# A fused two-layer attention kernel on one core: five seams reordered, the first context half put ahead of a batch's first scores in cross-attention, and a third fold of self-attention's sums on GpSimd

## The reference

```python
# layer 0: cross-attention to a projected memory, gated, then a norm
mem = einsum('bme,de->bmd', memory, W_mem)
ctx = softmax(x @ mem.T / sqrt(512)) @ mem
gate = sigmoid(concat([x, ctx]) @ W_gate + b_gate)
x = rmsnorm(x + gate * ctx)
# layer 1: each token takes one of two expert weights, chosen by a mask (vm)
q, k, v = split(where(vm, n(x) @ v_qkv, n(x) @ l_qkv)); q, k = rotary(q, k)
x = x + where(vm, c @ v_dense, c @ l_dense)        # c: causal self-attention, 16 heads of 32
x = x + cross(n(x) @ cq_w, context @ ckv_w) @ cdense_w     # 16 heads of 16, 375 keys
x = x + where(vm, mlp_v(n(x)), mlp_l(n(x)))        # silu(gate) * up @ down, 1376 wide
```

## Time and profile before

| | |
|---|---|
| median of 3 runs | 2148.39 us (2144.62 to 2150.19) |
| the profiled execution's own time | 2143.99 us |
| its span, first to last instruction | 2142.2 us |
| TensorE busy | 2093.4 us, 98% of the span |
| VectorE, ScalarE, GpSimd busy | 58%, 49%, 44% |
| mean granted TensorE clock | 0.993 of full speed |

### The profile page before, as it was taken

One profiled execution on the slowest core, in us unless ns is written; L12 is line 12 of the kernel. 1 busy time (PEld: TensorE's weight loads), 2 busy tenths in 40 slices (PEclk: granted clock), 3 DMA queues, 4 the chain that ended last, 5 costly groups with the idle time before them and its releaser, 6 DMA issues.

```text
span 2142.2 us, 40674 instructions
## 1 busy us (share of the span) xinstructions
PE 2093.4 (98%) x16042; PEld 1805.2 (84%) x16042; DVE 1237.3 (58%) x1908; ACT 1050.2 (49%) x1877; POOL 943.5 (44%) x773
## 2 busy tenths in 40 slices
PE   8999999999999999999999999989999999999998
PEld 7899998888777778887888888878888888888888
DVE  6665547657589975456666666663434435344343
ACT  5444435343378865534666565553443434433334
POOL 2211127776668854551111211115455554555447
PEclk9999999999999999998999999999999999999999
DMA  6443435655666655567877777745335343443334
GB/s 248 140 158 115 144 134 177 228 204 212 212 202 181 186 189 216 227 201 212 238 235 210 226 217 222 207 132 188 116 122 174 112 140 111 131 142 118 115 89 134
DMA packets 155742, 373.00 MB, mean 174 GB/s; under 512 B 40384, under 2 KB 61216, under 8 KB 145824
## 3 DMA queue, kind: packets, MB, share of 16 engines
q1 hardware_dynamic: 136400, 310.18, 45.8%
q0 software_dynamic: 18720, 60.04, 7.6%
q10 hardware_dynamic: 432, 0.17, 0.0%
HBM read 268.70 MB, written 100.46 MB: 172 GB/s over the span
## 4 chain that ended last, share of the span: by engine, by line
PE 83%; DMA 5%; DVE 3%; POOL 3%; SPq 2%; ACT 2%; issue 1%; POOLq 0%; DVEq 0%; ACTq 0%
PE ps L111 20%; PE ps L113 20%; PE ps L112 20%; PE ps L2017 4%; PE ps L2038 4%; PE ps L2051 3%; PE ps L1332 2%; PE ps L689 2%; PE ps L1321 1%; PE ps L1343 1%; DMA f_arena<-weights 1%; POOL cq_rows L1569 1%; PE ps L1311 1%; DMA cq_rows<-f_arena 1%; ACT f_arena L1595 1%
## 5 line engine op out<-in xcount | busy, mean ns | idle before, releaser
L111 PE MATMUL ps<-r_arena 128*128 128x512 f32 (+6 forms) x2410 | 890.9, 370 | 14.0 <-DVE r_arena L179 8.9
L113 PE MATMUL ps<-r_arena 128*128 128x512 f32 (+6 forms) x2410 | 880.0, 365 | 0.0
L112 PE MATMUL ps<-r_arena 128*128 128x512 f32 (+6 forms) x2410 | 879.6, 365 | 0.0
L179 POOL TENSOR_TENSOR r_arena<-f_arena,r_arena 128x512 fp32r<-128x512 f32 (+1 forms) x434 | 576.7, 1353 | 542.1 <-ACT r_arena L201 397.3
L111 PEld LDWEIGHTS ps<-r_arena 128*128 128x128 f32 (+2 forms) x2410 | 453.1, 188 | 79.0 <-POOL r_arena L179 6.7
L113 PEld LDWEIGHTS ps<-r_arena 128*128 128x128 f32 (+2 forms) x2410 | 452.7, 188 | 64.9
L112 PEld LDWEIGHTS ps<-r_arena 128*128 128x128 f32 (+2 forms) x2410 | 453.7, 188 | 59.3
L201 ACT CAST r_arena<-f_arena 128x512 fp32r<-128x512 f32 x400 | 236.4, 624 | 172.5 <-PE ps L113 127.3
L2159 DVE TENSOR_REDUCE e_negmax<-ps 112x3 f32<-112x1125 f32 (+1 forms) x192 | 229.9, 1198 | 113.1 <-PE ps L2017 113.0
L2476 DVE SCALAR_TENSOR_TENSOR f_arena<-f_arena,ps 128x512 f32<-128x512 f32 (+1 forms) x88 | 57.5, 653 | 233.8 <-ACT f_arena L2363 233.8
L1906 ACT ACTIVATE f_arena<-ps 125x896 f32<-125x896 f32 x192 | 165.4, 915 | 35.6 <-PE ps L2038 33.0
(11 more groups left out here) (215 smaller groups left out, 2575.4 us busy)
## 6 DMA issues: line engine op xcount, KB each, us to landing
f_arena<-weights SPq DMA_DIRECT2D x400, 256.0 KB, 3.0
r_arena<-k_rows SPq DMA_DIRECT2D x192, 188.0 KB, 3.6
k_rows<-r_arena SPq DMA_DIRECT2D x64, 376.0 KB
f_arena<-rows SPq DMA_DIRECT2D x14, 1160.0 KB, 5.2
f_arena<-qk_rows SPq DMA_DIRECT2D x32, 448.0 KB, 4.1
f_arena<-mem_n SPq DMA_DIRECT2D x8, 1536.0 KB, 6.8
f_arena<-mem_e SPq DMA_DIRECT2D x32, 376.0 KB, 4.9
f_arena<-mem_t SPq DMA_DIRECT2D x16, 750.0 KB, 5.5
```

Source lines behind the costliest of these rows:

```text
L111: first = pe.matmul(out, w_hi, x_hi, start=start, stop=False)
L112: pe.matmul(out, w_hi, x_lo, start=False, stop=False)
L113: return first, pe.matmul(out, w_lo, x_hi, start=False, stop=stop)
L179: return engine.tensor_tensor(out, source, high.bitcast(F32), ALU.subtract)
```

## The change

**Setup and phase A.** GpSimd clears the pad block before it turns to work that waits for group 0. VectorE works out the pads' slots in `setup_dve_places`, ahead of the softmax of group 1, and leaves the tiles' jumps (`setup_dve_jumps`) until after it. In group 0 the gate's four steps are interleaved with the four `attended` copies of group 1, which came after the third and fourth step before. For group 1, one half of the normed tokens comes earlier and one piece of splitting later.

**B to C.** The value rows of the last tile count on a semaphore of their own, so GpSimd issues them without waiting for the tile before. The two probability buffers swap places, and the wait for the older scatters passes from batch 0 to batch 1.

**Phase C, every step.** `turn_queries(s + 2)` moves ahead of the transposes on TensorE, and the copy of those queries ahead of the four copies on ScalarE. Block j=1 of the transposes now waits for the copy of these same queries. In 18 of 32 batches GpSimd adds a third fold (112 x 224), and VectorE's sum reads half as much.

**Phase E.** At its head 17 small matmuls that nobody reads (`keep_busy`) are put into three steps, the products for batch 3 are split around the second batch's first scores, and one unit of batch 0 gets another bank. In every step the first context half goes ahead of u=0. At the end the places of the last batch are issued by SyncE and ScalarE, three each, and the transposed maxima of batch 29 come before a context half.

```diff
@@ setup_pool, setup_dve_places @@
                 if m == C_GATE:
+                    pool.memset(tok[:, 0:PADS, :], 0.0).then_inc(pads_zeroed, 1)
...
                     pool.wait_ge(a_m_lo, 2 * CT)
                 ring_low(pool, m)
-            pool.memset(tok[:, 0:PADS, :], 0.0).then_inc(pads_zeroed, 1)
...
+            one_by_one(dve, dve.tensor_tensor(pad_slot[:], pad_m, grid, ALU.add))
+            dve.wait_ge(pads_zeroed, 2)
+            dve.tensor_scalar(tok[:, 0:PADS, ID].bitcast(I32), grid, float(TOKENS), None, ALU.add).then_inc(slots_made, 1)
             dve.wait_ge(s_rank, 2)
             dve.tensor_copy(place, ps[:, 5, 352:366]).then_inc(ranks_made, 1)
+
+        def setup_dve_jumps(dve):
@@ gated @@
+                copies = KT - 1 if g else 0
                 for t in range(KT):
-                    if t == KT - 1 and g + 1 < GROUPS:
+                    if t == copies and g + 1 < GROUPS:
                         for b in range(2):
                             attended(g + 1, b)
...
+                    if g == 0 and t in (1, 2):
+                        attended(1, t + 1)
@@ b_pool @@
+                    done = b_v_scattered if n + 1 < TILES else b_last_scattered.sem
+                    pool.indirect_dma_start(v_rows, ids, b_values(n, j), None).then_inc(done, 16)
...
-            pool.wait_ge(b_v_scattered, 16 * blocks(TILES - 1))
             store_v(TILES - 1)
@@ c_pool, fold @@
+                if b in c_thrice:
+                    pool.tensor_tensor(c_fold, c_half[:, :, 0:quarter], c_half[:, :, quarter:half], ALU.add).then_inc(c_halved.sem, 1)
+                    pool.wait_ge(*c_halved.at(c_halves(b) + 1))
+                    pool.tensor_tensor(c_eighth, c_fold[:, :, 0:quarter // 2], c_fold[:, :, quarter // 2:quarter], ALU.add).then_inc(
+                        c_folded.sem, 1)
@@ c_act @@
+                if s + 2 < BATCHES:
+                    queries(s + 2)
                 if s:
                     for j in range(QUADS):
                         act.wait_ge(c_pt, QUADS * (s - 1) + j + 1)
...
-                if s + 2 < BATCHES:
-                    queries(s + 2)
@@ c_pe @@
-                if j in (1, 2):
-                    pe.wait_ge((c_q, c_k)[j - 1], min(b + 3, BATCHES))
+                if j == 1:
+                    pe.wait_ge(c_q, min(b + 4, BATCHES))
+                if j == 2:
+                    pe.wait_ge(c_k, min(b + 3, BATCHES))
...
+                if s + 2 < BATCHES:
+                    turn_queries(s + 2)
                 if s >= 1:
                     for j in range(QUADS):
                         transposes(s - 1, j)
-                if s + 2 < BATCHES:
-                    turn_queries(s + 2)
@@ c_dve @@
-                dve.tensor_reduce(c_sum[:], c_fold, AX_X, ALU.add).then_inc(c_summed, 1)
+                dve.tensor_reduce(c_sum[:], c_eighth if b in c_thrice else c_fold, AX_X, ALU.add).then_inc(c_summed, 1)
@@ e_sp, e_act @@
+                if b == BATCHES - 1:
+                    place_last(sp, last_places[:3])
+                    return
...
+                if s == BATCHES - 2:
+                    act.wait_ge(e_st, KEY_UNITS * (BATCHES - 3))
+                    place_last(act, last_places[3:])
@@ e_pe @@
+            def keep_busy(bank, count):
+                for _ in range(count):
+                    pe.matmul(ps[0:SEQ, bank, 0:NT], ident_b[0:SEQ, 0:SEQ], causal[:].rearrange("p m s -> p (m s)"),
+                              start=True, stop=True)
...
+                if old:
+                    context(s - 2, 0)
                 if now:
                     scores(s, 0)
...
                 if old:
-                    context(s - 2, 0)
```

More of the change, by code:

```diff
@@ L858, in a_dve @@
                         x_low(g + 1)
-                    means(g - 1, 1)
-                    tokens(g - 1, 0)
+                    if g == 1:
+                        tokens(g - 1, 0)
+                        means(g - 1, 1)
+                        memory_low(g + 1, 1)
+                    else:
+                        means(g - 1, 1)
+                        tokens(g - 1, 0)
                     tokens(g - 1, 1)
@@ L877, in a_dve @@
                     if g == 0:
+                        setup_dve_jumps(dve)
                         setup_dve_slots(dve)
@@ L1166, in c_sp @@
                 load_qk(b)
-            sp.wait_ge(b_v_scattered, 16 * BLOCKS)
+            sp.wait_ge(b_v_scattered, 16 * blocks(TILES - 1))
+            sp.wait_ge(*b_last_scattered.at(16 * tb(TILES - 1)))
             for b in range(3):
@@ L1197, in fold @@
                 if b == 0:
-                    pool.wait_ge(b_v_scattered, 16 * BLOCKS)
+                    pool.wait_ge(b_v_scattered, 16 * blocks(TILES - 1))
+                    pool.wait_ge(*b_last_scattered.at(16 * tb(TILES - 1)))
                 if b:
@@ L1772, in place_queries, with place_last @@
                     e_placed[b].sem, 16)
+        def place_last(engine, parts):
+            b = BATCHES - 1
+            engine.wait_ge(*stored(b))
+            into, done = e_queries[b % 3].rearrange("p t g s -> p t (g s)").bitcast(F32), e_placed[b % 2].sem
+            for t, part in parts:
+                engine.dma_start(rows_of(into, t, part)[:, t], q_rows[b, t, (0, 0, 1)[part]]).then_inc(done, 16)
+        last_places = [(t, part) for t in range(CT) for part in range(3)]
         def e_sp(sp):
@@ L2105, in e_pe @@
                     f_gate_up(pe, 0, 0, 0, (0, 1, 2))
-                if by_key:
+                if by_key and s != BATCHES - 2:
                     maximum_turn(s - 1)
@@ L2116, in e_pe @@
                     scores(s, 2)
-                if new and s:
+                if s == 1:
+                    keep_busy(6, 2)
+                    queries_turn(3)
+                    keep_busy(6, 2)
+                if new and s >= 2:
                     e_key_products(pe, s + 2)
```

78 lines of the change are left out of this document (49 added, 29 removed).

## The result

The changed kernel takes 2153.16 us in the median of 7 runs (2152.68 to 2155.55), the kernel before 2147.28 (2144.62 to 2150.19, 7 runs). The ratio is 1.003, with a 95% interval of 1.0021 to 1.0039: slower by 5.9 us, where the forecast was 2152 with a sum of +3.5. The profiled execution of the changed kernel took 2152.73 us, 8.74 more than the profiled one of before; the medians stand closer because the profiled execution of before lies 3.29 under its kernel's median, and no other execution of it has a trace.

What follows compares the result with a forecast made beforehand. TensorE's program was taken to set the time in phase C. Terms 10.2 - 4.5 - 1.3 - 2.9 + 3.6 - 1.6 = +3.5 us on the median 2148.39 gave 2152 us; 8 in 10 from 2139 to 2163.

Steps and rivals of the forecast that it cites:

- Phase C: Self-attention steps: block j=1 waits for the queries' copy, starting 1.22 us after X, the queries' start; +0.35 a step, +10.2 us.
- The first rival: Phase C: the copy of the queries is hidden after all, gaining 2.9 us; 2139 us, chance 0.20.
- The third: Rival in phase C: TensorE drops to the lower clock, +80 us, to 2230; chance 0.02.
- Phase A: Interleaved copies remove TensorE's stop at 66 us and the load issued at 71.55 quickens without pad scatters beside it; -4.5 us.
- the second rival: Phase A: the load issued at 71.55 stays slow, so the 4.5 us is lost; 2156, up to 2163; chance 0.28.
- B to C: Seam before phase C's first context: value rows scattered earlier, first subtraction moves up too; -1.3 us.
- the 0.84 goes: At the first context of phase C: the 0.84 us wait for value rows disappears because they are scattered earlier.
- Head of E: Start of phase E: added matmuls keep the clock up and places are issued earlier; -2.9 us.
- if the 17 added matmuls keep the clock up: Head of phase E: 1.2 us won in the context and about as much in the products before.
- E's steps: Every step of phase E: hidden wait -0.16, shape changes +0.18, new wait for the maximum +0.13; +3.6 us in all.
- two changes of tile shape: Each step of phase E: the new order adds two shape changes at 0.09 us each, 0.18.
- Tail of E: End of phase E: a context half fills batch 31's 1.37 us wait for places and two engines issue; -1.6 us.

Runs made afterwards that it cites:

- x4: The kernel before with only the new order of queries and transposes in phase C, on TensorE and ScalarE; 2156.28 us, ratio 1.0054.
- x2: The changed kernel with banks 5 and 7 swapped for the second and third block of transposes in phase C; 2144.19 us, ratio 0.999.
- x3: The changed kernel without GpSimd's third fold, VectorE's sum reading what two folds leave; 2153.02 us, ratio 1.0026.
- a2: The kernel before with only phase A's interleaved copies, the pads scattered as late as before; 2149.54 us, ratio 1.0015.
- x6: The changed kernel with all six places of the last batch's queries issued by SyncE again; 2152.99 us, ratio 1.0026.
- x7: The changed kernel without the 17 added matmuls at the head of phase E; 2153.3 us, ratio 1.0034.
- a1: The kernel before with only the setup part, pads cleared, placed and scattered earlier, gate and copies in the old order; 2145.76 us, ratio 0.9998.

## Why the prediction was right

The time, 2153.16, lies 1 us from the forecast, and the sign was right. That it lies so near is in part luck: the forecast started from a median of three runs, 2148.39, 1.1 above the 2147.28 of seven, and its sum of +3.5 was 2.4 under the 5.9 measured; and inside the sum one term missed by 3.5 us and one by 2.2. What carried the sign, the loss in every step of C, was right. By its steps:

- **Phase C: right in place, mechanism and size.** Forecast +0.35 a step and +10.2; measured 0.38 a step and +10.7 (10.6 in x4). The chain of rows gave the start of the second block within 0.01 us (X + 1.22 against 1.23). What it put a little too low was the end: the last block's copy ended at 687.32 + 1.40 = 688.72, X + 3.26 (forecast 3.24), but the context took another 0.38 us behind it, where one quarter of it and the handover had been put at 0.28. In all the context ended 0.12 later than forecast; the rest of the step made good most of it, 0.10 shorter where 0.02 had been taken, so the step's 0.38 beside 0.35 owes something to two errors that cancel. x2 shows that the bank decides, x3 that GpSimd and VectorE don't. The first rival, a hidden copy, is refuted by the bracket itself. The third, a lower clock through the phase, is refuted by the clock of 1.00 in that stretch. The Trainium skill, page "TensorE: Matmul & The Clock Gate", Part 4 on PE-mode transpose, says that transposes don't count as busy in the same way, and this phase with 28 transposes a step and a stall in each doesn't show it.
- **Phase A: right in size, half right in its reason.** Forecast -4.5, measured -4.8 at 90 us. The slow load was there (4.71 from issue at 71.53 to first use in the changed kernel, against 8.97), so the second rival, a load that stays slow, falls. But a2 shows the step that failed: it named the load as the only thing behind TensorE's stop, and the wait for the pad scatters' own landing is another.
- **B to C: right in size, wrong in mechanism.** Forecast -1.3, measured -1.2, and -1.2 to -2.1 in the other eight executions with the new seam. The step that failed is "the 0.84 goes": the first context waits for value rows as before, now for 1.72 us (1.1 to 1.8 in the others). Counted from 575 us, the first of these rows landed 1.2 us sooner, and TensorE was through with its own work 2.1 sooner. The longer stop has a price that the forecast didn't see: behind it the clock fell in x3, x6 and x7 (mean 0.54, 0.77 and 0.77 from 591.5 to 599 us, against 1.00 in the changed kernel's trace), and from the first context to 790 us those three lost 12.3 to 13.7 us in place of 10.7. x4, with the old seam, has such a fall ahead of its first context (0.86 from 590 to 602 us), so it isn't the new seam's alone.
- **Head of E: the term was too large.** Forecast -2.9, measured -0.7, and between executions the head varies by more than that. The step that failed is the price set on "if the 17 added matmuls keep the clock up". They kept it up for a part only: it was 0.50 to 0.53 from 965 to 975 us, 1.00 to 985, and 0.66 from 985 to 990, where the context stands from which the 1.2 was read. Its two halves took 2.04 and 1.29 us there, 0.42 less than the 3.75 from 983.52 to 987.27 in the kernel before (the 3.72 of the earlier trace rows is a row of 92 of the 96 products). And where the clock was up, TensorE waited for other engines.
- **E's steps: right in place and mechanism, near in size.** Forecast +3.6, measured +3.0. Of the parts, the hidden wait was 0.15 (forecast 0.16) and the new wait 0.11 (0.13, in which the handover of 0.05 was taken off where it has to be added). What the forecast called two changes of tile shape, 0.18, shows as 0.09 on the scores by key (0.96 against 0.87) and 0.15 on the parted context halves; that the change of shape is the reason is argued, and no run tests it. The parts come to +0.20, and the step grew by 0.12: what gives 0.08 back in the rest of the step is open.
- **Tail of E: wrong.** Forecast -1.6, measured +1.9. The step that failed is that it looked at the wait for batch 31's queries, which is indeed gone, and put nothing on the smaller one 7 us ahead of it, for the place of batch 29's maxima (0.57 us in that trace). That one is a race with a load of 1 MB in the queue ahead of it: it took 0.81 us in the changed kernel's trace and up to 5.65 in others, and TensorE came back from it at the lower clock. How far the change's own earlier turn of the maxima makes it worse is open.

The two errors at E's ends, +2.2 and +3.5, are the whole gap between the sum of +3.5 and the 8.7 of the profiled pair, with small ones against them elsewhere.

## What to carry to other kernels

Before a step is moved ahead of another, look at which bank each writes: two that share one are tied by the copy between them, and moving the first in front of the second puts that copy on TensorE's path once a step, here 0.38 us net of the 0.10 that was gained. Swapping the banks took 0.35 of the 0.38 away. A wait that is removed alone can show nothing when a second limit lies right behind it (a1 and a2 gained 0.5 and nothing, together 4.8), so try the parts of such a seam together before dropping either. And where a seam ends on a DMA, moving up the work ahead of it can just lengthen the stop: at the first context of C the wait doubled while the seam gained what was forecast.

## What the runs showed that was not expected

A DMA of 14 KB behind a 1 MB load on the same queue kept TensorE waiting for anything from 0.30 to 5.65 us, on the whole longer where it was issued sooner behind the load (3.65 down to 1.83 us), and TensorE's scores by key took 1.66 to 2.02 us after every wait of 1.34 or more, in place of 1.13 in the kernel before. One profiled execution is therefore a poor yardstick for a seam that ends on such a DMA; the steady steps of one kernel's loops repeated within 0.01 us, taken as an average, from one execution to the next.
